# Perceiver kernel: quantised layer tile by tile, absorbed weights made inside it, second context attention's front reordered, experts over groups of four tiles

## The reference

```
def bitlinear(x, w):
    x_q = activation_quant(x)      # round(x * 127/max|x|), clipped, over the scale
    w_q, scale = weight_quant(w)   # clip(round(w / mean|w|), -1, 1)
    return einsum('bsd,hd->bsh', x_q, w_q) * scale
h = new_gelu(bitlinear(x, w1))     # 256 -> 1024
return bitlinear(h, w2)            # 1024 -> 256
```

```
for e in range(16): acc += (silu(x @ w1_e) * (x @ w3_e)) @ w2_e * coef[:, e]
out = (silu(x @ s1) * (x @ s3)) @ s2 * sigmoid(x @ sgate) + acc
```

## Time and profile before

| | us |
|---|---|
| median of 3 runs (3134.65 to 3139.06) | 3134.79 |
| the profiled execution, its own time | 3134.59 |
| its span, first to last instruction | 3132.8 |

### The profile page before, as it was taken

The page is one execution under the profiler, slowest core; times in us unless marked ns, Lnnn a source line. Parts: engine busy times, 40 slices in busy tenths (PEclk is TensorE's granted clock), DMA queues, the critical chain, the costliest instruction groups (busy, mean ns, idle before and its releaser), DMA issues. The chain is left out here.

```text
span 3132.8 us, 50156 instructions
## 1 busy us (share of the span) xinstructions
PE 2743.6 (88%) x17688; PEld 1779.7 (57%) x17688; DVE 1573.3 (50%) x2714; ACT 1269.2 (41%) x2578; POOL 1234.1 (39%) x656
## 2 busy tenths in 40 slices
PE   6878345599999999999999999999969899999998
PEld 4656224464556455545554655465426577777776
DVE  4756676246445644654465446544529633333332
ACT  4557122134433544444445444544425433333332
POOL 1011000347667766776677657766740000000000
PEclk9989656689999999999999999999979999999999
DMA  1000300111110110111111011101030000000000
GB/s 44 1 16 0 131 0 0 62 42 40 43 38 27 53 42 27 38 53 38 31 38 53 30 39 38 53 27 43 16 161 0 1 1 0 0 0 0 0 0 27
DMA packets 26585, 98.12 MB, mean 31 GB/s; under 512 B 3808, under 2 KB 8544, under 8 KB 25120
## 3 DMA queue, kind: packets, MB, share of 16 engines
q1 hardware_dynamic: 24864, 94.15, 9.1%
q10 hardware_dynamic: 1664, 3.18, 0.3%
HBM read 55.71 MB, written 2.10 MB: 18 GB/s over the span
## 5 line engine op out<-in xcount | busy, mean ns | idle before, releaser
L755 POOL TENSOR_TENSOR cx_acc<-cx_acc,cx_prob 128x1024 f32<-128x1024 f32 (+1 forms) x352 | 835.1, 2373 | 396.6 <-ACT cx_prob L1043 389.2
L1043 ACT ACTIVATE cx_prob<-cx_st 128x512 f32<-128x512 f32 (+1 forms) x832 | 477.5, 596 | 539.4 <-PE cx_st L883 518.1
L1140 DVE TENSOR_REDUCE cx_mhalf<-cx_mx 128x1 f32<-128x804 f32 x512 | 485.7, 987 | 217.8 <-PE cx_mx L859 217.7
L894 PE MATMUL cx_av<-cx_prob,cx_kv 128*64 128x512 f32 (+1 forms) x1664 | 453.6, 624 | 0.0
L882 PE MATMUL cx_st<-cx_q,cx_k 128*128 128x512 f32 (+1 forms) x832 | 368.0, 442 | 42.6 <-ACT cx_prob L1043 42.0
L1606 PE MATMUL moe_gu<-moe_wgu,moe_xnT 128*128 128x352 f32 x1280 | 398.1, 462 | 0.0
L859 PE MATMUL cx_mx<-cx_kp,cx_q 128*128 128x402 f32 x1024 | 303.0, 379 | 62.5 <-DVE cx_mhalf L1140 59.2
L883 PE MATMUL cx_st<-cx_q,cx_k 128*128 128x512 f32 (+1 forms) x832 | 332.8, 400 | 0.0
L859 PEld LDWEIGHTS cx_mx<-cx_kp,cx_q 128*128 128x128 f32 x1024 | 174.1, 193 | 248.2 <-DVE cx_mhalf L1140 186.7
L1606 PEld LDWEIGHTS moe_gu<-moe_wgu,moe_xnT 128*128 128x128 f32 x1280 | 241.8, 191 | 124.4 <-issue 6.7
L1741 DVE SCALAR_TENSOR_TENSOR moe_hid<-moe_silu,moe_coef,moe_gu 128x176 f32<-128x176 f32 x320 | 126.9, 397 | 350.9 <-ACT moe_silu L1669 349.0
(11 more groups left out here) (210 smaller groups left out, 3667.9 us busy)
## 6 DMA issues: line engine op xcount, KB each, us to landing
cx_k<-cx_kp SPq DMA_DIRECT2D x32, 804.0 KB, 3.9
cx_ctx<-in_cx_ctxN SPq DMA_DIRECT2D x32, 416.0 KB, 3.2
cx_ctxr<-in_cx_ctxrN SPq DMA_DIRECT2D x32, 416.0 KB, 4.1
cx_k<-cx_kp SPq DMA_DIRECT2D x32, 402.0 KB, 5.2
moe_wgu<-in_moe_wgu SPq DMA_DIRECT2D x5, 1408.0 KB, 13.6
moe_wd<-in_moe_wd SPq DMA_DIRECT2D x4, 896.0 KB, 24.8
x_all<-in_x SPq DMA_DIRECT2D x1, 2048.0 KB, 4.0
cx_wq<-in_cx_wq SPq DMA_DIRECT2D x1, 2048.0 KB, 12.0
```

The costliest lines, as they stand in the source:

```text
L755: pool.tensor_tensor(acc[rows, :, :], sofar, prob[slot(kt)][rows, :, :], ALU.add).then_inc(s_acc, 1)
L894: last = pe.matmul(av[DCX * p:DCX * p + DCX, :], kv[e][0:nk(kt), kt, :], prob[slot(kt)][0:nk(kt), p, :], start=(kt == 0), stop=(kt == NKT ...
L1043: act.activation(prob[slot(kt)][rows, p, :], st[p][rows, :], ACT.Exp).then_inc(s_exp, 1)
L1140: dve.tensor_reduce(mhalf[:, i // 2, i % 2:i % 2 + 1], mx[i % 2][:, :, 0:KQ], AX.XY, ALU.max)\
```

## The change

**Quantised layer.** The load block goes: SP issues `w2`, then `w1`, then the six raw matrices, then the three tables, and DVE waits for each weight matrix by itself, `w2` first. Scaling and rounding of the weights go to ACT; DVE clips once, between ROUND-1 and ROUND+1. The main block goes tile by tile, unrolled: rounding of the hidden values on ACT (`round_hidden`), one clipping pass on DVE instead of two, fewer small steps, the addition to `x` on POOL. **Absorbed weights** are made in the same block, 32 jobs over one bank `made`, PE in two places of each tile and ACT copying; from the fourth half tile on. `rotated` does its wide and its narrow pieces apart. The separate block and the tables' load go.

```
+            for m, (w, q, lo, n, width) in enumerate(order):      # DVE, order: w2, w1
+                dve.wait_ge(s_load[m], 16)
+                step.done(dve.tensor_reduce(sc, w, AX.X, ALU.add, apply_absolute_value=True))
...
+                dve.reciprocal(rc, sc).then_inc(s_scale, 1)
+            for m, (w, q, lo, n, width) in enumerate(order):
+                for i in range(n):
+                    last = dve.tensor_scalar(diag[:, lo + i, :], ident, asum[...], None, ALU.mult)
+                last.then_inc(s_diag, 1)
+                dve.wait_ge(s_scaled, m + 1)
+                dve.tensor_scalar(w, w, ROUND + 1.0, ROUND - 1.0, ALU.min, ALU.max).then_inc(s_clip, 1)
...
+            for m, (w, q, lo, n, width) in enumerate(order):      # ACT
+                act.wait_ge(s_scale, m + 1)
+                for i in range(n):
+                    last = act.activation(w[:, i, :], w[:, i, :], ACT.Identity, bias=bias[:, 0:1], scale=rec[...])
+                last.then_inc(s_scaled, 1)
+                act.wait_ge(s_clip, m + 1)
+                act.activation(q, w, ACT.Identity, bias=bias[:, 1:2]).then_inc(s_q, 1)
...
+    JOBS_AT = 3
+    first = lambda k: max(0, k - JOBS_AT) * len(jobs) // (2 * NT - JOBS_AT)
...
+            def make(n):                                          # PE
+                product, j, _, _, kind = jobs[n]
+                pe.wait_ge(*arrived[kind])
+                if n > 0:
+                    pe.wait_ge(s_keep, n)
+                product(pe, made, j).then_inc(s_made, 1)
+            for t in range(NT):
+                for n in job_range(t, 0):
+                    make(n)
+                turn_y2(t)
+                for n in job_range(t, 1):
+                    make(n)
+                down_product(t)
+                if t + 2 < NT:
+                    turn_y1(t + 2)
+                    up_product(t + 2)
...
+            for t in range(NT):                                   # ACT
+                round_hidden(t)
+                if t + 1 < NT:
+                    gelu(t + 1)
+                for n in job_range(t, 0):
+                    keep(n)
+                keep_y2T(t)
+                for n in job_range(t, 1):
+                    keep(n)
+                if t + 2 < NT:
+                    keep_y1T(t + 2)
...
+            for t in range(NT):                                   # DVE
+                find_scale(t)
+                if t + 1 < NT:
+                    unscale(t + 1)
+                quantise_hidden(t)
+                if t + 2 < NT:
+                    quantise_x(t + 2)
+                if t > 0:
+                    change_x(t - 1)
+                if t + 3 < NT:
+                    gather(t + 3)
+            # POOL: update_x(t - 1), then root(t + 3)
```

**Context attention's front.** The tables are there. The order of every engine changes:

```
             def before():                                         # POOL
+                root(0)
+                rotate(0, 0); rotate(0, 1); sum_keys(0); keep_kl(0)
+                rotate(1, 0); rotate(1, 1); sum_keys(1)
+                pool.wait_ge(s_kr, 2)
                 ... memsets ...
-                root(0)
-                for n in range(2):
-                    rotate(n, 0); rotate(n, 1); sum_keys(n); keep_kl(n)
                 root(1)
+                keep_kl(1)
             def before():                                         # PE
-                pe.wait_ge(s_set, 6)
-                pe.wait_ge(s_one, 1)
-                for r in range(KROUNDS):
-                    turn_keys(0, r)
                 turn_x(0)
                 for j in range(0, CP + 2, 2):
...
+                    if j >= 4:
+                        turn_keys(0, j // 2 - 2)
+                turn_keys(0, KROUNDS - 1)
                 for i in range(PIECES):
                     max_scores(0, 0, 0, i)
-                for r in range(KROUNDS):
-                    turn_keys(1, r)
+                    if i % 4 == 3:
+                        turn_keys(1, i // 4)
+                pe.wait_ge(s_set, 6)
+                pe.wait_ge(s_one, 1)
                 max_rows(0, 0)
```

```
+            for g in range(NG):                                   # PE, k over NFC = 28 chunks
+                for k in range(NFC):
+                    gate_product(g, k)        # group 0: gate and up of chunks 0 and 1 ahead,
+                    share_product(g, k)       # then turn_coefficients(0)
+                    up_product(g, k)
+                    down_product(g, k - 2)
+                    # next group: turn_x at 9 and 11, router at 14, turn_coefficients at 21
...
+            def gated_product(g, k):                              # DVE
+                dve.wait_ge(s_silu, n + 1)
+                dve.wait_ge(s_share, n + 1)
+                dve.tensor_tensor(gated, silu, share, ALU.mult).then_inc(s_gated, 1)
+            def hidden(g, k):
+                dve.wait_ge(s_up, n + 1)
+                dve.tensor_tensor(hidT, gated, up, ALU.mult).then_inc(s_hid, 1)
...
+            # DVE's queue: both for each chunk; gather at 3, 4, normalise at 6, 7, logits at 14,
+            # ranks at 16, split at 18; update_x(g - 1) at 1. share_product(n) waits for gated n - 1.
```

More of the change, by code:

```diff
@@ L1484, in _, with scales @@
[L1484 to L1486 removed]
+            step.start(0)
+            def scales(t, col):
+                step.done(dve.tensor_scalar(back[t % 2][:, col:col + 1], amax[t % 2][:, col:col + 1], 1e-5, 1.0 / 127.0,
+                                            ALU.max, ALU.mult))
+                return dve.reciprocal(inv[t % 2][:, col:col + 1], back[t % 2][:, col:col + 1])
@@ L1489 @@
+            change_x(NT - 1)
 E, TOPK, FE = 16, 4, 176
@@ L1649, in _, with down_product @@
-            turn_x(0, 0)
-            router(0, 0)
-            rounds(pe, tile)
+                last.then_inc(s_up, 1)
+            def down_product(g, k):
+                n = chunk(g, k)
+                pe.wait_ge(s_hid, n + 1)
+                if k == 0 and g > 0:
+                    pe.wait_ge(s_x, g * GT)
+                for i in range(GT):
+                    last = pe.matmul(acc[:, i, :], hidT[n % RING][:, i * P:(i + 1) * P], wd[:, k, :],
+                                     start=(k == 0 and i % 2 == 0), stop=(k == NFC - 1), skip_group_check=True)
+                last.then_inc(s_down, 1)
@@ L1762, in _, with gather @@
-            normalise(0, 0)
-            logits(0, 0)
-            coefficients(0, 0)
-            rounds(dve, tile)
+            step.start(0)
+            part = [parts[:, :, i * CE:(i + 1) * CE] for i in range(PARTS)]
+            def gather(g, half):
+                for i in (2 * half, 2 * half + 1):
+                    last = dve.bn_stats(stats[:, i, :], x_all[:, g * GT + i, :])
+                step.done(last)
+                for i in (2 * half, 2 * half + 1):
+                    dve.memset(mv[:, i, 2:3], 0.0)
+                    last = dve.bn_aggr(mv[:, i, 0:2], stats[:, i, :])
+                step.done(last)
+                tiles = mv[:, 2 * half:2 * half + 2, 1]
+                dve.tensor_scalar(tiles, tiles, EPS, None, ALU.add).then_inc(s_var, 1)
```

962 lines of the change are left out of this document (541 added, 421 removed).

## The result

The kernel after the change takes 3007.71 us (median of four runs, 3004.69 to 3018.13), the one before 3136.93 beside it: ratio 0.9594, 95% interval 0.9569 to 0.9619. The profiled execution spans 3005.6 us, 127.2 less than the one before; a time of 3005 was predicted. The page of the kernel after: busy time by engine, and the granted clock in 40 slices.

What follows compares the result with a forecast made beforehand. Three limits: PE bounds the experts, dependencies round DVE the quantised layer, PE's wait for keys the context front. From 3134.6 us, -92.6 (quantised layer and absorbed weights), -21.8 (front) and -14.8 (experts) gave 3005 us; range 2984 to 3034.

Steps and rivals of the forecast that it cites:

- Part 1: Quantised layer's weights: loading, scaling and rounding end at 347.1 instead of 358.5 us, gain 11.4 us, bounds -3 and +3.
- Part 2: Quantised layer's tiles: period 7.7 us, between 8.7 at a slow clock and 6.6 at a fast one; tiles gain 38 us.
- Rival (a): Quantised layer: the clock stays low and `rotated` jobs add 6 us; +25 us, kernel 3030; chance 0.20.
- rival (b): Quantised layer: jobs keep the clock up and DVE sets a 6.7 us period; -15 us, kernel 2990; chance 0.18.
- I take half of each: Quantised layer's tiles: period put at 7.7 us, midway between the slow clock's 8.7 and the fast clock's 6.6.
- Rival (d): Quantised layer: the jobs don't fit the gaps and delay the chain of waits by 37 us; kernel 3042; chance 0.08.
- The ring for the fast clock: Quantised layer's tiles: the cycle of waits between engines at 2.4 GHz, put at 6.4 us, below DVE's own 6.6.
- POOL at 0: Quantised layer: moving the addition to `x` to POOL was taken to cost 0 us.
- The 12 us bound: Quantised layer: the most that POOL's addition to `x` could cost, 0.73 us a tile, 12 us in all.
- Part 3: Context attention's front: reordered work reaches first scores in 54.6 us instead of 76.4, gain 21.8, bounds 15 and 25.
- Part 4: Experts and store: PE-bound chunks of 5.38 us, 112 making 603 us, and a shorter final store; gain 14.8 us.
- between the front and the experts nothing is edited: Stages from context front to experts (648 to 2480 us): taken as unedited, with a predicted change of 0.

Runs made afterwards that it cites:

- e5: Kernel after the change with the experts' spreading product issued twice in each chunk; 3030.38 us, ratio 0.9663.
- e6: Kernel after the change with the experts, their weights' arrays and the single store of the kernel before; 3019.46 us, ratio 0.9628.
- e1: Kernel after the change with all 32 absorbed-weight jobs behind the last tile, none in the tiles before; 3084.28 us, ratio 0.9819.
- e2: Kernel after the change with the same 32 jobs in the same gaps, in turn big, rotated, big, values; 3001.46 us, ratio 0.9561.
- e7: Kernel after the change with the work ahead of the first context batch in the order of the kernel before; 3031.23 us, ratio 0.9670.
- e11: Kernel after the change with `change_x` of the tile before put ahead of `quantise_x` on VectorE; 3008.07 us, ratio 0.9585.
- e10: e8 with each of its 24 `big` and `values` products issued twice into the same bank; 2986.70 us, ratio 0.9505.
- e3: Kernel after the change with the quantised layer's addition to `x` back on VectorE from GpSimd; 3007.04 us, ratio 0.9587.
- e4: Kernel after the change with the experts' 14 load issues moved from the rotary attention's loading block to the next block; 3000.97 us, ratio 0.9570.
- e9: e8 with the 8 `rotated` jobs behind the last tile and the other 24 spread over the gaps; 3019.85 us, ratio 0.9619.
- e8: Kernel after the change with e4's edit, one job in each of 32 gaps, and half of `w1`'s scaling on VectorE; 2988.95 us, ratio 0.9535.
- e12: e8 with e11's order and each `values` product issued three times; 2979.70 us, ratio 0.9498.

## Why the prediction was right, and where it was not

**Part 1** was right to 0.5 us. `w2`'s reduction began 4.9 us after its issue (5.2). The pieces of `w1` were mis-sized: eight of 256 columns took ACT 4.02 us, 0.5 each, not 0.35; DVE waited 4.43 us for them. Shorter copies made up for it.

**Part 2, its period** was right as a mean, 7.60 for 7.7, and so was the reason that the granted clock decides between two rings; rivals (a) and (b) were the two ends of it. What failed was "I take half of each": it is no half state. Seven periods took 6.98 to 7.00 us (rival (b) had 6.7); the first two had a granted clock of 0.50 and most others one between, with 1.2 GHz for a part of the tile. Which tiles do differs between executions, 157.7 or 168.3 us for the stage. Rival (a) at 3030 supposed the low clock everywhere; its mechanism, tiles held up by `rotated` jobs at 1.2 GHz, is what happened in e5 and e6 from 430 to 468 us. Rival (d), all jobs adding to the ring, is refuted by e1, but its mechanism is there in two gaps: where two jobs stand before `turn_y2`, the next period took 8.0 us at the full clock in the kernel after, and in the eight traces with this spacing (the kernel after, e2 to e7, e11) the periods behind these two gaps took 8.0 to 10.1 and 10.0 to 13.7 us. My sum spread 2.2 jobs evenly over each tile. The Trainium skill's rule (TensorE: Matmul & The Clock Gate, What's actually happening) that the low clock is the default and activity releases it agrees with e1 (0.60) and e10 (0.98), but the window of e6, busy 90% at 0.53, shows that busy time alone does not.

The ring for the fast clock, 6.4 us, left out that `down` waits for `change_x`; with DVE's 6.6 (measured 6.53) as the larger, the error was hidden and came to 0.4 us a tile.

**POOL at 0** was right as far as e3 can tell. The 12 us bound, and the rule that stood behind it, found nothing to bite on in these tiles; VectorE's `tensor_scalar` of `xn` took 404 to 412 ns there.

**Part 3** was too low by 5.4 us. `big` at +3.2 (3.5) and `max_scores` at +28.8 (31) were close; the rest took 20.4 us, not 23.6. Of this the sixteen pieces took 17.4, which I had put at 20: the key turns of the second batch (0.6 to 1.06 us) fell in PE's waits for VectorE's reductions, which I had not counted as cover, `normalise` took 0.41 us there and waited for nothing, and the granted clock was 0.71 (0.54 before). How much each of the three gave is not separated. e7 shows that the order did all of the gain.

**Part 4** was too low by 5.4: 2.5 for router and turns (3 x 0.8), 1.2 at the end (updates and store 4.8 us instead of 6.0), 1.0 by the chunks, 0.5 in group 0, where the stall was 1.7 shorter and the slow start cost 1.2 more, and 0.1 by the first gate. e5 shows that a chunk is PE alone.

**The step that failed is the sentence "between the front and the experts nothing is edited".** True of the code, not of the queue: 14 issues on SyncE instead of 11, with 1.8 MB more, end a block 5.2 us later (e4, e6). I had counted DMAs in the quantised layer and not here. The 4.7 us ahead of the quantised layer are no part of the change: TensorE's products of one of the first tiles took nearly twice as long in this execution (eight `a_wq` products 2.07 us instead of 1.16, sixteen `a_kbd` ones 1.99 instead of 1.09), and other runs with the same code there reached the quantised layer at 319.5. The 1.8 us in the batches are within what runs with the same code there show, 1662.9 to 1672.3 us for that stage; their cause is open.

**Open:** what makes the clock dip in single tiles. It isn't the `rotated` jobs alone (e9), and filling helps (e10). The longest tiles stand behind a gap with two jobs, and e8, e9, e10 and e12, in which no gap holds two different jobs, have no period above 8.7 us; but no run changes this alone. Nor does any run undo the tile-by-tile order or the lighter passes of VectorE by themselves, so how the tiles' gain is shared among them is not shown.

## What to carry to other kernels

Independent products laid into the gaps of a loop that is bound by waits paid twice here: they were hidden, and they held TensorE's clock up for the chain that crosses it. Judge them by the granted clock of that window as well as by the room in the gaps, and put no second one into a gap if it must first wait for the copy of the one before. Forecast a loop that stands between two clocks as two prices with a count of each, never as their mean. And where a block ends only when a queue has issued everything, each DMA added to it can cost its issue time there, wherever its data is used: issue bulk loads from the block after.

## What was not expected of the hardware

- Throwaway products shortened a loop: 15 periods 110.3 to 104.6 us, granted clock 0.86 to 0.98 (e8, e10).
- A window with PE busy 34.16 of 38.00 us had a granted clock of 0.53 (e6), one with 50.66 of 74.20 had 0.94 (kernel after).
- The same stage of unchanged code took 157.7 or 168.3 us in different runs, each pattern repeated to 0.2 us a tile.
- The time that SyncE takes to issue a DMA does not follow the size of the load. In the kernel after, the eleven loads of the quantised layer, up to 2 MB each, took 0.33 to 0.65 us to issue; in the rotary attention each `moe_wgu` piece (1 MB) took 0.6, each `moe_wd` piece (0.9 MB) 0.9 and the 1.8 MB `moe_owner` 2.11, behind the others. The same `moe_wd` pieces, with two loads fewer ahead of them, took 0.5 each in the kernel before.
